# A one-core audio tower: x loaded in three parts, first heads split by batch, token statistics moved to GpSimd, and staged reads placed between the stores

## The chip, the cores and the metric

The kernel runs on one core of a Trainium2 chip. The time is the device time of one launch in microseconds. Before the change it is 169.0 us, the median of three runs (167.67 to 170.44).

## The reference

x is (16, 4000): 16 signals. Three stages follow each other; what is computed, cut to what matters:

```python
# 1 token stage: interpolate x by 4, windows of 64, 250 tokens of 64 per signal
kw = 0.5*(w + 1.3)**2 + 0.5*exp(-0.5*(w - 0.7)**2)
M = abs(fft(kw)); Mmax = M.max(-1)
h = soft_minimum(M * sigmoid(M - 0.12*Mmax), 0.9*Mmax)
# 2 attention, 8 heads of 64, sigmoid instead of softmax
q, k, v = (layernorm(h) @ W for W in (Wq, Wk, Wv))
h = h + relu((sigmoid(q @ k.T * 8) @ v) @ Wo)
# 3 shared MLP and 4 experts, two of them chosen by a softmax gate
y = layernorm(h)
out = h + shared(y) + sum_of_top2(gates(y), experts(y))
```

A token's 64 values are symmetric (bins 1 to 31 mirror 33 to 63), so the kernel works with 33 of them in stage 1 and with 32 folded features in the score and value products. The folded weights are products made on the chip.

## The kernel before

There are 16 signals, two to a **pair** g (0 to 7), each with 250 tokens in two interleaved halves of 125: four rows of `tok` to a pair, 32 in all. The rows are handled in groups `first` (0 to 7, pairs 0 and 1), `third` (8 to 15, pairs 2 and 3) and `later` (16 to 31, pairs 4 to 7). All engines run their own instruction lists, strictly in the written order, and meet at semaphores.

**Stage 1.** x comes as 36 taps by 2000 columns (`tapsT`), in two loads of 500 and 1500 columns (line 232), after memsets on VectorE (line 649) and GpSimd (line 1160). SyncE then issues the loads of the attention weights (233) and the FFN weights (234); ScalarE issues three loads of constants (1032 to 1034). Four quarters of 500 columns go through interpolation (TensorE, 289), square and exponential (ScalarE, 1040, 1042), two sums (VectorE, 653, 657) and the Fourier product (TensorE, 297). Magnitudes, masks and tokens follow (`over`, `distance`, `soft_minimum`), then a layer norm by the steps `total`, `centre`, `square`, `total`, `variance` (lines 711 to 732) on VectorE and a power of -0.5 on GpSimd (`inverse_deviation`, 1167), and the split of the normalised rows into two float16 parts (`split_rows`, 1172, on GpSimd; for pair 0 on VectorE, 750).

**Stage 2.** For a pair g: `x_transpose(g)` on TensorE, `x_take(g)` on VectorE copies to XT; then queries projected by head. For pair 0 this is `y_pair(p)` for four pairs of heads into banks 2 to 5 (372), whose high float16 part is taken by ScalarE (`pair_high`, 1090) and whose low part by VectorE (`pair_low`, 893). For other pairs it is `y_project(g, k)` for two halves of the heads k (361), `y_take(g, k)` on VectorE (769, 771), a store to DRAM (`send`, 242) and four reads that bring it back in another layout into YS (`read_back`, 255), all issued by SyncE in one order: store 0, store 1, reads 0, reads 1. Then there are eight units n for each pair: `scores(n)` (389 for pair 0, 398 else), the sigmoid on ScalarE (1110), `mix(n)` (418), emitted two units later; units 0 to 3 of a pair use the first half of the heads. `z_take(g, u)` copies what two units mixed. `mix` writes banks 4 and 5. The main loop (471) scatters the transposes, projections and `attn_out` of other pairs between the units.

**What ties pairs together.** `attn_out(g)` is added to the tokens by `add_attention(g)` on VectorE (782). It waits for `mirrored` 2: GpSimd copies the mirrored half of the tokens (1232) for rows 0 to 15 and then 16 to 31. `x_transpose(g)` for g >= 4 shares bank 7 with it and waits for `h2_done` >= g - 3 (344), that is for `add_attention(g - 3)`. GpSimd's list before the change: powers and split for pair 1, packing of the score weights, splitting of the FFN weights (1212 to 1224), powers and splits for pairs 2 and 3, one power for all later rows, the two mirrored copies, then splits of pairs 4 to 7 and the second layer norm (`norm2`).

**Stage 3** begins at about 105 us: layers 1 to 3 of the experts and the shared part on TensorE, pair by pair.

## Time and profile before

| what | value |
|---|---|
| median of three runs | 169.0 us |
| profiled execution: time, span | 168.07 us, 166.3 us |
| granted TensorE clock, mean | 0.974 |
| busy TensorE | 150.9 us (91%) |
| busy ScalarE, VectorE, GpSimd | 114.2, 109.5, 50.2 us |
| staged queries: stores, reads | 14 of 250 KB, 56 of 125 KB |

The profiled execution is the one that the rows come from; its time is the span and 1.77 us around it. A busy share over the whole span mixes the three stages; the stages are best read one by one, as the rows further down do. PE stands for TensorE, PEld for its weight loads, DVE for VectorE, ACT for ScalarE, POOL for GpSimd, SP for SyncE.

### The profile page before, as it was taken

How to read it: one execution, taken by the hardware profiler on the slowest of the kernel's cores; microseconds unless marked ns; L12 is line 12 of the kernel's file. 1: busy time of each engine (PE TensorE's matmuls, PEld its weight loads, DVE VectorE, ACT ScalarE, POOL GpSimd, SP SyncE). 2: the span in 40 equal slices, each digit the busy share in tenths (PEclk: the TensorE clock that was granted, in tenths of full speed). 3: DMA queues.
4: the chain of work that ended last, by engine and by line, in shares of the span. 5: the costliest groups of instructions: out<-in, count | busy, mean ns of one | idle time of the engine just before them, and what ended most of it. 6: DMA issues, size and time to landing. Idle time of an engine off the chain costs nothing.

```text
span 166.3 us, 6649 instructions
## 1 busy us (share of the span) xinstructions
PE 150.9 (91%) x2824; PEld 90.4 (54%) x2824; DVE 109.5 (66%) x277; ACT 114.2 (69%) x156; POOL 50.2 (30%) x94
## 2 busy tenths in 40 slices
PE   7799695996998999999989999999999999999890
PEld 2278531443454667575646455544666565765580
DVE  2396998996686767767681949777359884443521
ACT  3498973996877897978877898647636627457420
POOL 4000019692932855463416162526100000000000
PEclk9999659999999999999999999999999999999997
DMA  5920000058277685929576800000000100101002
GB/s 144 197 101 0 4 0 0 0 158 216 91 197 220 161 210 134 239 73 236 150 200 167 189 6 4 4 0 0 4 23 14 33 9 26 31 4 35 21 17 59
DMA packets 14701, 14.03 MB, mean 84 GB/s; under 512 B 1288, under 2 KB 14444, under 8 KB 14608
## 3 DMA queue, kind: packets, MB, share of 16 engines
q1 hardware_dynamic: 14240, 13.25, 30.5%
q8 instruction: 22, 0.36, 0.9%
q10 hardware_dynamic: 432, 0.36, 0.9%
q14 instruction: 7, 0.06, 0.1%
HBM read 9.00 MB, written 4.60 MB: 82 GB/s over the span
## 4 chain that ended last, share of the span: by engine, by line
PE 43%; DMA 21%; DVE 12%; SPq 11%; ACT 8%; issue 3%; DVEq 0%
DMA y_stage<-YP 14%; SPq L255 11%; PE ps L516 8%; PE ps L534 7%; PE ps L573 7%; PE ps L418 5%; PE ps L398 5%; DMA YS<-y_stage 4%; PE ps L543 3%; DMA area<-x_in 3%; PE ps L558 2%; PE ps L429 2%; ACT probs L1110 1%; PE ps L454 1%; ACT area L1046 1%
## 5 line engine op out<-in xcount | busy, mean ns | idle before, releaser
L1110 ACT ACTIVATE probs<-ps 125x1000 f32<-125x1000 f32 x64 | 61.6, 1007 | 11.8 <-PE ps L398 10.4
L418 PE MATMUL ps<-probs,xn 124*32 124x250 f32 (+1 forms) x512 | 39.0, 375 | 0.0
L398 PE MATMUL ps<-YS,XT 128*32 128x500 f16 x448 | 34.1, 376 | 3.4 <-DMA YS<-y_stage 3.2
L418 PEld LDWEIGHTS ps<-probs,xn 124*32 124x32 f32 (+1 forms) x512 | 15.6, 109 | 12.2 <-issue 1.5
L1140 ACT ACTIVATE H2r<-ps,wf 128x500 f32<-128x500 f32 x16 | 10.8, 677 | 15.4 <-PE ps L534 15.4
L779 DVE COPY ZS<-ps 128x250 f32<-128x250 f32 x32 | 12.9, 414 | 11.0 <-PE ps L418 10.8
L398 PEld LDWEIGHTS ps<-YS,XT 128*32 128x32 f16 x448 | 10.4, 96 | 12.3 <-DMA YS<-y_stage 4.5
L979 DVE TENSOR_TENSOR area<-H2r,ps 128x500 f32<-128x500 f32 x16 | 10.8, 674 | 9.2 <-ACT H2r L1140 8.6
L534 PE MATMUL ps<-area,wf 128*64 128x500 f32 x64 | 16.7, 585 | 0.0
L1127 ACT ACTIVATE area<-ps,wf 128x500 f32<-128x500 f32 x24 | 15.9, 672 | 0.9 <-PE ps L516 0.9
L1169 POOL TENSOR_TENSOR norm<-norm,half_neg 125x4 f32<-125x4 f32 (+1 forms) x5 | 6.9, 1397 | 26.7 <-DVE norm L732 26.7
L573 PE MATMUL ps<-wf,area 128*61 128x64 f32 (+1 forms) x384 | 14.0, 225 | 0.0
L573 PEld LDWEIGHTS ps<-wf,area 128*64 128x64 f32 (+1 forms) x384 | 13.2, 136 | 0.6
L970 DVE TENSOR_SCALAR area<-ps,wf 128x500 f32<-128x500 f32 (+1 forms) x16 | 9.5, 604 | 6.0 <-PE ps L516 5.8
L769 DVE CAST YP<-ps 128x500 f16<-128x500 f32 x12 | 8.1, 677 | 7.7 <-PE ps L361 7.7
L516 PE MATMUL ps<-X2T,w1h 128*64 128x500 f16 x64 | 12.9, 382 | 0.0
L516 PE MATMUL ps<-X2T,w1l 128*64 128x500 f16 x64 | 12.7, 373 | 0.0
L1186 POOL TENSOR_TENSOR lnsq<-ln 125x256 f32<-125x256 f32 x8 | 4.9, 612 | 25.3 <-DVE ln L796 25.3
L771 DVE TENSOR_TENSOR YP<-ps,YP 128x500 f16<-128x500 f32 x14 | 9.5, 678 | 1.0 <-issue 0.3
L279 PE MATMUL ps<-warm 128*128 128x512 f16 x20 | 8.2, 578 | 1.0 <-POOL warm L1159 1.0
L429 PEld LDWEIGHTS ps<-outW,ZS 128*32 128x32 f32 (+1 forms) x512 | 8.2, 109 | 1.5 <-issue 0.4
L429 PE MATMUL ps<-outW,ZS 128*32 128x64 f32 (+1 forms) x512 | 8.7, 219 | 0.0
(151 smaller groups left out, 247.6 us busy)
## 6 DMA issues: line engine op xcount, KB each, us to landing
YS<-y_stage SPq DMA_DIRECT2D x56, 125.0 KB, 3.0
y_stage<-YP SPq DMA_DIRECT2D x14, 250.0 KB, 4.0
tower_out<-res SPq DMA_DIRECT2D x8, 124.0 KB
wf<-wf_in SPq DMA_DIRECT2D x1, 648.0 KB, 7.3
wa<-wa_in SPq DMA_DIRECT2D x1, 512.0 KB, 6.5
area<-x_in SPq DMA_DIRECT2D x1, 210.9 KB
ch<-ch_in ACTq DMA_DIRECT2D x1, 160.0 KB, 4.9
cf<-cf_in ACTq DMA_DIRECT2D x1, 128.5 KB, 2.6
```

Source lines behind the costliest of these rows:

```text
L255: sp.dma_start(YS[row:row + R, g % 3, 4 * k:4 * k + 4, :], src).then_inc(y_in[g % 3][k], 16)
L398: last = mm(ps[k0:k1, 2 * (n % 2) + j, 0:TG].rearrange("p (h n) -> p h n", h=2), XT[:, g % 3, (2 * bb + cj) * P + k0:(2 * bb + cj) * P + k ...
L418: last = mm(ps[R * hh:R * hh + R, 4 + bb, half * TB:(half + 1) * TB], xn[0:keys, 4 * g + 2 * bb + cj, :], probs[0:keys, n % 3, hh, :], sta ...
L429: last = mm(ps[q0:q1, 7, t * F:(t + 1) * F], ZS[:, g % 2, half, t * P + q0:t * P + q1], outW[:, half, :], start=(half == 0), stop=(half == 1))
L516: last = mm(ps[F * c:F * c + F, n % 3, 0:TG], w[:, e * 128 + F * c:e * 128 + F * c + F], X2T[:, g, :], start=(k == 0), stop=(k == 1))
L534: last = mm(ps[F * j:F * j + F, 3 + k, 0:TG], wf[:, WF["w2"][0] + e * F:WF["w2"][0] + (e + 1) * F], H1[:, g % 2, e, :], start=True, stop=True)
L573: last = mm(ps[q0:q1, OUT_BANK[g], t * F:(t + 1) * F], H2[:, g % 2, k, t * P + q0:t * P + q1], wf[:, WF["w3"][0] + k * F:WF["w3"][0] + (k ...
L779: v.tensor_copy(ZS[:, g % 2, half, bb * TB:(bb + 1) * TB], ps[:, 4 + bb, half * TB:(half + 1) * TB]).then_inc(z_cp, 1)
L979: v.tensor_tensor(H2[:, g % 2, k, :], H2r[:, g % 2, k, :], ps[:, 5, 0:TG], ALU.mult).then_inc(mix_done, 1)
L1110: fn(probs[:, n % 3].rearrange("p (j h) n -> p j (h n)", j=2), ps[0:P, 2 * (n % 2):2 * (n % 2) + 2, 0:TG], ACT.Sigmoid, scale=SCORE_SCALE) ...
L1127: fn(H1[:, g % 2, e, :], ps[:, n % 3, 0:TG], ACT.Relu, bias=wf[:, WF["b1"][0] + e:WF["b1"][0] + e + 1]).then_inc(l1_act, 1)
L1140: fn(dst, src, ACT.Relu, bias=wf[:, WF["b2"][0] + k:WF["b2"][0] + k + 1]).then_inc(l2_act, 1)
```

## The change

Six things are done at once.

1. x comes in three loads (500, 500, 1000 columns). The loads of attention weights, `ch` (which ScalarE issued before) and FFN weights go out by SyncE behind the landing of the third.
2. For the first rows the variance step is gone: epsilon is added within `total`, the power is taken of the sum and a factor of 8 is multiplied in later.
3. The queries of pair 0 come in six parts: head pairs 0 and 1 are split by signal (parts 0 to 3, 250 columns, banks 2 to 5), head pairs 2 and 3 (parts 4 and 5, 500 columns, banks 4 and 5 again) are projected after unit 1. Their copies on ScalarE go behind sigmoids 1 and 2.
4. Projections and transposes for pairs 1 to 3 are placed up to two units earlier, `attn_out(0)` one later.
5. Tokens of the later rows and squares of the third and later rows are computed on GpSimd (VectorE and ScalarE before). Order on VectorE and GpSimd is new, as the diff shows: powers and splits of pairs 2 to 4 stand ahead of the splitting of the FFN weights.
6. SyncE's order is store 0 of a pair, reads 1 of the pair before, store 1, reads 0. In the FFN `layer3` of the last pair but one is emitted earlier.

The diff, cut to its core:

```diff
-PAIR_BANK = (2, 3, 4, 5)
+PARTS = ((0, 0, 2), (1, 0, 3), (0, 1, 4), (1, 1, 5), (2, None, 4), (3, None, 5))
+TAP_COLS = (slice(0, 4 * P), slice(4 * P, 8 * P), slice(8 * P, NB * P))
...
+            sp.wait_ge(taps_in[2], 16)
             sp.dma_start(wa[:], wa_in).then_inc(attn_w_in, 16)
+            sp.dma_start(ch[:], ch_in).then_inc(const16_in, 16)
...
-            for g in range(1, NG):
-                for k in range(2):
-                    send(g, k)
-                for k in range(2):
-                    read_back(g, k)
+            send(1, 0)
+            send(1, 1)
+            read_back(1, 0)
+            for g in range(2, NG):
+                send(g, 0)
+                read_back(g - 1, 1)
+                send(g, 1)
+                read_back(g, 0)
+            read_back(NG - 1, 1)
...
# TensorE
+            def y_part(i):
...
+                if i >= 4:
+                    pe.wait_ge(yd_lo, i - 1)
...
-                        pe.wait_ge(yd_lo, pair + 1)
+                        pe.wait_ge(yd_lo, (5 if half else 3 if bb else 1) + i)
...
-                if n == 0:
-                    pe.wait_ge(yd_lo, 3)
-                if n == 2:
-                    pe.wait_ge(yd_lo, 4)
+                if n in (0, 2):
+                    pe.wait_ge(yd_lo, 5 + n // 2)
...
-                if n in (0, 1):
-                    y_project(1, n)
-                if n == 6:
+                if n == 0:
+                    for k in range(2):
+                        y_project(1, k)
+                if n == 1:
+                    for i in (4, 5):
+                        y_part(i)
+                if n == 5:
                     x_transpose(2)
-                if n in (7, 8):
-                    y_project(2, n - 7)
-
-                if t == (3 if g == 1 else 1) and 1 <= g < NG - 2:
+                if n in (6, 7):
+                    y_project(2, n - 6)
+
+                if t == (2 if g == 1 else 1) and 1 <= g < NG - 2:
                     x_transpose(g + 2)
...
-                if t == (4 if g == 1 else 3) and g >= 1:
+                if t == (5 if g == 1 else 3) and g >= 1:
...
# VectorE
-            total(first, masked)
-            variance(first)
+            total(first, masked, F * EPS)
+            dve1_at["squares", first.start] = st.n
...
             x_take(0)
             total(third, tok)
+            for i in range(2):
+                part_low(i)
+            x_take(1)
+            for i in range(2, 4):
+                part_low(i)
             centre(third)
...
             y_take(1, 0)
+            dve.wait_ge(square_pool, 1)
             total(third, masked)
             variance(third)
+            part_low(4)
             y_take(1, 1)
+            part_low(5)
 
             z_take(0, 0)
-            soft_minimum(later)
+            x_take(2)
+            z_take(0, 1)
+            y_take(2, 0)
+            y_take(2, 1)
+            z_take(0, 2)
+            dve.wait_ge(token_pool, 1)
             total(later, tok)
...
             centre(later)
...
+            z_take(0, 3)
+            x_take(3)
+            z_take(1, 0)
+            y_take(3, 0)
+            dve.wait_ge(square_pool, 2)
             total(later, masked)
             variance(later)
...
# ScalarE, after sigmoid n
+                if n in (1, 2):
+                    part_high(n + 3)
                 if n in (0, 1):
                     second_high(n)
-                if n == 6:
-                    act.wait_ge(dve1, dve1_at["centred", later.start])
-                    fn(masked[:, later, :], mag[:, later, 0:NBIN], ACT.Square).then_inc(square_done, 1)
...
# GpSimd, behind the packing of the score weights
+            pool.wait_ge(act1, 6)
+            v.tensor_tensor(tok[:, later, 0:NBIN], masked[:, later, :], dist[:, later, :],
+                            ALU.subtract).then_inc(token_pool, 1)
...
+            square_rows(third)
+            inverse_deviation(slice(8, 12), third)
+            split_rows(2)
+            inverse_deviation(slice(12, 16), third)
+            split_rows(3)
+            square_rows(later)
+            inverse_deviation(slice(16, 20), later)
+            split_rows(4)
             pool.wait_ge(ffn_w_in, 16)
             v.tensor_copy(w1h[:], wf[:, 0:E * 128 + F + E]).then_inc(w1_split, 1)
...
-            inverse_deviation(slice(8, 12), third)
-            split_rows(2)
-            inverse_deviation(slice(12, 16), third)
-            split_rows(3)
-            inverse_deviation(later, later)
+            inverse_deviation(slice(20, 32), later)
+            pool.wait_ge(dve1, dve1_at["token", third.start])
             for rows in (slice(0, 16), later):
-                pool.wait_ge(dve1, dve1_at["token", later.start if rows == later else third.start])
                 v.tensor_copy(tok[:, rows, NBIN:F], tok[:, rows, NBIN - 2:0:-1]).then_inc(mirrored, 1)
```

## Rows read from the trace of the kernel before

**Rows 1.** Stage table: us; busy PE, PEld, DVE, ACT, POOL (count); clock; DMA share; GB/s.
```profile
59.00:105.00 46.00, 44.83 (x1160) 26.93 (x1145) 31.48 (x91) 39.44 (x45) 20.25 (x37) 1.00 0.55 141
```
**Rows 2.** Timeline, TensorE: starts of pairs 1 to 6 and x_transpose(4); start, us, instruction, idle before.
```profile
40.31 0.61 PE L398 MATMUL ps<-YS,XT 128*32 128x500 f16 x8 [1.31 <-DMA YS<-y_stage]
...
50.42 0.61 PE L398 MATMUL ps<-YS,XT 128*32 128x500 f16 x8 [0.92 <-DMA YS<-y_stage]
...
52.13 0.39 PE L350 MATMUL ps<-ch,xs 125*32 125x125 f16 x16
...
59.01 0.60 PE L398 MATMUL ps<-YS,XT 128*32 128x500 f16 x8
...
67.73 0.60 PE L398 MATMUL ps<-YS,XT 128*32 128x500 f16 x8
...
76.98 0.61 PE L398 MATMUL ps<-YS,XT 128*32 128x500 f16 x8 [0.35 <-DMA YS<-y_stage]
...
86.37 0.61 PE L398 MATMUL ps<-YS,XT 128*32 128x500 f16 x8 [0.63 <-DMA YS<-y_stage]
```
**Rows 3.** Timeline, the four quarters of the interpolation on TensorE and VectorE.
```profile
5.85 0.68 DVE L653 SCALAR_TENSOR_TENSOR area<-ps,square 128x500 f32<-128x500 f32 x1 [3.96 <-ACT square L1040]
6.40 2.78 PE L289 MATMUL ps<-area,cf 128*128 128x500 f32 x6 [1.21 <-DMA area<-x_in]
...
8.17 0.68 DVE L653 SCALAR_TENSOR_TENSOR area<-ps,square 128x500 f32<-128x500 f32 x1 [0.91 <-ACT square L1040]
...
9.48 0.67 DVE L653 SCALAR_TENSOR_TENSOR area<-ps,square 128x500 f32<-128x500 f32 x1
```
**Rows 4.** Timeline, the variance step on VectorE (third rows).
```profile
33.08 0.17 DVE L732 TENSOR_SCALAR norm<-norm 125x8 f32<-125x8 f32 x1
```
**Rows 5.** Timeline, first scores: VectorE's steps and TensorE's units of pair 0.
```profile
28.01 0.46 DVE L722 SCALAR_TENSOR_TENSOR mag<-norm,tok 125x264 f32<-125x264 f32 x1
...
28.39 1.25 DVE L893 TENSOR_TENSOR YS<-ps,YS 128x500 f16<-128x500 f32 x2
...
31.85 0.63 PE L418 MATMUL ps<-probs,xn 125*32 125x250 f32 x8
...
32.35 0.16 DVE L714 TENSOR_TENSOR norm<-masked 125x8 f32<-125x8 f32 x1
...
34.18 0.41 DVE L779 COPY ZS<-ps 128x250 f32<-128x250 f32 x1
...
35.11 0.64 PE L389 MATMUL ps<-YS,XT 64*125 64x250 f16 x8
...
36.24 0.64 PE L389 MATMUL ps<-YS,XT 64*125 64x250 f16 x8
```
**Rows 6.** Timeline, GpSimd: weight splitting (first, last), pair 3 (first, last), power, mirrored copies.
```profile
28.13 0.87 POOL L1212 CAST w1h<-wf 128x580 f16<-128x580 f32 x1
...
31.90 0.18 POOL L1224 COPY wg<-w1l 128x4 f16<-128x4 f16 x1
...
36.03 1.01 POOL L1169 TENSOR_TENSOR norm<-norm,half_neg 125x4 f32<-125x4 f32 x1
...
38.10 0.43 POOL L1182 TENSOR_TENSOR xs<-xn,xs 125x128 f16<-125x128 f32 x1
41.97 2.90 POOL L1169 TENSOR_TENSOR norm<-norm,half_neg 125x16 f32<-125x16 f32 x1 [3.44 <-DVE norm L732]
44.82 1.14 POOL L1232 COPY tok<-tok 125x496 f32<-125x496 f32 x2
```
**Rows 7.** TensorE's clock: stage table of 17.7 to 24.4, and timeline of three stretches.
```profile
17.70:24.40 6.70, 6.26 (x41) 3.40 (x42) 6.14 (x16) 6.11 (x11) 0.02 (x1) 0.50 0.01 2
...
18.14 1.98 PE L320 MATMUL ps<-wkT,wqT 64*128 64x64 f32 x16 [1.83 <-ACT wkT L1070]
...
0.98 3.38 PE L279 MATMUL ps<-warm 128*128 128x512 f16 x8 [0.98 <-POOL warm L1159]
...
27.31 1.02 PE L372 MATMUL ps<-XT,scoreW 128*128 128x500 f16 x4 [0.53 <-DVE XT L760]
```

More of the change, by code:

```diff
@@ L180, in build @@
             sem(s) for s in ("interp_in", "const_in", "const16_in", "attn_w_in", "ffn_w_in"))
-        taps_in = [sem(f"taps_in{q}") for q in range(2)]
+        taps_in = [sem(f"taps_in{q}") for q in range(3)]
         w16_set = sem("w16_set")
@@ L190, in build @@
         xn_pool = sem("xn_pool")
[L191 to L192 removed]
+        xs0_done, xs_pool, half_set, square_pool, token_pool, rstd_done = (
+            sem(s) for s in ("xs0_done", "xs_pool", "half_set", "square_pool", "token_pool", "rstd_done"))
         xt_mm, xt_cp, y_mm, y_hi, y_lo = (sem(s) for s in ("xt_mm", "xt_cp", "y_mm", "y_hi", "y_lo"))
@@ L363, in y_project @@
                 last.then_inc(y_mm, 1)
-            def y_pair(p):
-                if p == 0:
+            def y_part(i):
+                p, b, bank = PARTS[i]
+                cols = columns_of(b)
+                if i == 0:
                     pe.wait_ge(xt_cp, 1)
@@ L467, in _ @@
             x_transpose(0)
-            for p in range(4):
-                y_pair(p)
+            for i in range(4):
+                y_part(i)
             x_transpose(1)
@@ L601, in _ @@
                     layer2(g, 1)
+                if g == NG - 1:
+                    layer3(g - 1)
                 if g + 1 < NG:
@@ L617, in _ @@
                     layer1(g + 1, 3)
-                if 1 <= g <= NG:
+                if 1 <= g <= NG and g != NG - 1:
                     layer3(g - 1)
@@ L709, in soft_minimum, with total @@
                     v.tensor_tensor(tok[:, rows, 0:NBIN], masked[:, rows, :], dist[:, rows, :], ALU.subtract))
-            def total(rows, of):
+            def total(rows, of, plus=0.0):
                 st.wait()
-                st.done(v.tensor_tensor(norm[:, 1, rows], of[:, rows, 0], of[:, rows, R], ALU.add))
+                if plus:
+                    st.done(v.scalar_tensor_tensor(norm[:, 1, rows], of[:, rows, 0], -plus, of[:, rows, R],
+                                                   ALU.add, ALU.add))
+                else:
+                    st.done(v.tensor_tensor(norm[:, 1, rows], of[:, rows, 0], of[:, rows, R], ALU.add))
                 st.wait(st.done(v.tensor_reduce(norm[:, 0, rows], of[:, rows, 0:NBIN], AX_X, ALU.add)))
@@ L749, in _ @@
             dve.wait_ge(rstd_done, 1)
-            st.wait(st.done(v.tensor_tensor(xn[:, rows, :], mag[:, rows, 0:R], wide(4, rows, R, norm), ALU.mult)))
+            st.wait(st.done(v.scalar_tensor_tensor(xn[:, rows, :], mag[:, rows, 0:R], float(F) ** 0.5, wide(4, rows, R, norm),
+                                                   ALU.mult, ALU.mult)))
             high, low, full = parts(rows)
@@ L1086, in second_high, with part_high @@
                 fn(YP[:, 1, 0, k, :], ps[:, y_bank(1, k), 0:TG], ACT.Copy).then_inc(y_hi, 1)
-            def pair_high(p):
-                act.wait_ge(yd_mm, p + 1)
-                fn(YS[:, 0, 2 * p, :], ps[:, PAIR_BANK[p], 0:TG], ACT.Copy).then_inc(yd_hi, 1)
-            for p in range(4):
-                pair_high(p)
+            def part_high(i):
+                p, b, bank = PARTS[i]
+                cols = columns_of(b)
+                act.wait_ge(yd_mm, i + 1)
+                fn(YS[:, 0, 2 * p, cols], ps[:, bank, cols], ACT.Copy).then_inc(yd_hi, 1)
+            for i in range(4):
+                part_high(i)
             def gate_sigmoids(r):
@@ L1200, in norm2 @@
                                 ALU.subtract).then_inc(x2s_done, 1)
-            inverse_deviation(slice(0, 4), first)
-            inverse_deviation(slice(4, 8), first)
+            pool.wait_ge(dve1, dve1_at["squares", first.start])
+            for g in range(2):
+                rows = slice(4 * g, 4 * g + 4)
+                v.tensor_tensor(norm[:, 4, rows], norm[:, 2, rows], half_neg[0:P, rows], ALU.pow).then_inc(rstd_done, 1)
+            pool.wait_ge(rstd_done, 2)
+            v.tensor_scalar(norm[:, 4, 4:8], norm[:, 4, 4:8], float(F) ** 0.5, None, ALU.mult).then_inc(rstd_done, 1)
             split_rows(1)
@@ L1209, in _, with square_rows @@
                               scoreW[:, :, 0, :].rearrange("p (i a j) r -> p i a j r", i=2, a=2)[:, :, k]).then_inc(packed, 1)
+            pool.wait_ge(act1, 6)
+            v.tensor_tensor(tok[:, later, 0:NBIN], masked[:, later, :], dist[:, later, :],
+                            ALU.subtract).then_inc(token_pool, 1)
+            def square_rows(rows):
+                pool.wait_ge(dve1, dve1_at["centred", rows.start])
+                v.tensor_tensor(masked[:, rows, :], mag[:, rows, 0:NBIN], mag[:, rows, 0:NBIN],
+                                ALU.mult).then_inc(square_pool, 1)
+            square_rows(third)
[6 more added lines that the diff above has]
+            split_rows(4)
             pool.wait_ge(ffn_w_in, 16)
```

49 lines of the change are left out of this document (18 added, 31 removed).

## The prediction, made before the change was built or timed

> **What bounds the kernel now.** I read the stage table first, then the timelines of each stage. From 59 to 105 us TensorE is busy 44.83 of 46.00 us and ScalarE 39.44 [rows 1]: there the kernel runs at TensorE's pace. One batch pair (eight score units) takes 67.73 - 59.01 = 8.72 us [rows 2]. What is not at this pace are the starts of pairs whose staged queries are late: pair 1 at 40.31, pair 2 at 50.42, pair 5 at 76.98 and pair 6 at 86.37 all sit behind "DMA YS<-y_stage" [rows 2]. Pair 1 lasts 50.42 - 40.31 = 10.11 us, pair 5 9.39. Ahead of 40 us a chain over all engines sets the time. So I follow three things: the chain to the first scores, the start of each pair, and what other engine can hold TensorE in pairs 1 and 2. All clock times below are on the old time axis; what the head saves is taken off at the end. The sum is made against the profiled execution, 168.07 us, which lies 0.93 under the median of 169.0.
>
> **Head.** Quarter 2 of the interpolation waits for a large load until 6.40, though quarter 1 was at VectorE at 5.85 and quarter 2 got there at 8.17. The pitch of a quarter on VectorE is 9.48 - 8.17 = 1.31 [rows 3]. With a load of its own, quarter 2 comes at 5.85 + 1.31 = 7.16: **-1.0**. Bounds: 0 if the small load lands no sooner, -1.2 if ScalarE's part also shrinks; the load is of the size of the first, so I take -1.0. The weights now leave after x has landed; the first that uses them is two engines off the chain, so I cost that at nothing (worst case some 0.5). Dropping the variance step of the first rows takes 0.17 and a hand-over off the chain [rows 4]: **-0.2**. The extra multiply on GpSimd is behind the first power and off this chain. Head: **-1.2**.
>
> **First scores.** VectorE has finished its sums at 28.01; it now subtracts for two half-width parts before centring instead of after. A 250-column operation takes 0.41 against 0.63 for each of the two full ones, which ended at 28.39 + 1.25 = 29.64 [rows 5]; parts 0 and 1 are ready at 28.42 and 28.8, 0.85 sooner, and so is the first sigmoid. But this is not kept. Mix 0 writes bank 4, and bank 4 now also holds part 4, so mix 0 waits for VectorE's fifth subtraction. In front of that stand on VectorE: second copy x_take(1), parts 2 and 3, centring (to 30.2), y_take(1,0) (to 31.4), the nine tenths of a microsecond of total and variance (32.35 to 33.25 now [rows 4, 5]; then 31.45 to 32.35), and part 4, 0.68: 33.05. The squares of these rows, now GpSimd's, are done by 31.0 and hold nobody. Mix 0 ran at 31.85; it will run at 33.05, and behind it TensorE goes at its own pace of 36.24 - 35.11 = 1.13 per unit [rows 5]. Through units 3 to 7 with one transposition and two projections (0.33 + 0.2 + 0.2) the ninth scores come at 33.05 + 0.57 + 4 x 1.13 + 0.8 + 0.85 = **39.8**, against 40.31. The data are there: its first projection is stored 1.0 earlier, at 31.4. Gain here only 0.5, and it is overrun by what follows.
>
> **The copies that the attention sum waits for.** This is the step that I think decides. add_attention(0) waits for `mirrored` 2, the two mirrored copies of the tokens on GpSimd; x_transpose(4), the second unit of pair 2, waits for add_attention(0). Now the copies end at 44.82 + 1.14 = 45.96, and TensorE comes to x_transpose(4) at 52.13 [rows 2, 6]: no wait. In the new order two things happen.
> VectorE computes the variance of the later rows not at 41.9 but behind z_take(0,3), x_take(3), z_take(1,0) and y_take(3,0). y_take(2,1) ends at 41.4, z_take(0,2) 41.75, total 42.7, centring 43.4, z_take(0,3) 43.8, x_take(3) 44.15, z_take(1,0) 44.5. The projection for y_take(3,0) was held by x_take(3) and is there at 44.6; two passes of 0.68 take it to 46.0; total and variance 1.2 more: **47.2**.
> GpSimd then has, before the copies: power of 4 columns and split_rows(4), 38.53 - 36.03 = 2.5; all of the splitting of the FFN weights, which used to be done at 28 to 32 and is now queued behind split_rows(4), 32.08 - 28.13 = 3.95; the power of 12 columns, between 1.01 for 4 and 2.90 for 16, by their slope 2.27; the copies, 1.14 [rows 6]. That is 9.86. Copies end at 47.2 + 0.1 + 9.9 = 57.2; add_attention 0.42: x_transpose(4) can start at **57.6** instead of 52.13: **+5.5**. TensorE would have reached it at about 51.7 and stands for six microseconds. VectorE stands too, with z_take(1,3) and x_take(4) behind the wait. Bounds: 56.2 if the second VectorE chain follows the ninth scores with no other wait (their start plus 6.3, then 10), 58.6 if the GpSimd rows stretch as the cast did (0.29 to 0.65).
>
> **After the wait.** At full clock one more 0.7 is lost, as y_project(4,0) waits for x_take(4), which VectorE reaches 1.75 after its release. But the clock will not stay full. [...] How long it lasts once work is back has two rows: 6.3 us behind 18.14, and at the launch the eight warm-up matmuls of 512 columns still went at 0.42 each for 3.38 us (the clock's column reads full there, so I go by their pace), against 0.25 for 500 columns at full clock [rows 7]. Half of such a stretch is lost: 1.7 to 3.1, and this swallows the 0.7. I take **+2.4**; both ends, and 0.7 for no fall at all, go into the range.
> [...] The 0.42 and 0.25 above agree with a halved pace.
>
> **Order of stores and reads.** SyncE now issues four reads between two stores instead of standing until a store has landed. Pairs 5 and 6 no longer start late. Pairs 4 and 5 lasted 9.25 and 9.39 instead of 8.72 [rows 2]: **-1.2**. Against it: the second half of the reads of pair 1 waits behind the first store of pair 2, which is ready only at 40.1; four issues and a landing of about 3 us bring the data at 45.3, and unit 12 would start at 44.6. That 0.7 lies ahead of the long wait and adds nothing to it, as GpSimd's chain starts from VectorE. In later pairs each read is some ten microseconds early.
>
> **Tail.** layer3 of the last pair but one fills a hole of 0.44 us, but the last one waits for a spread that moves behind it by 0.9; nothing, within 0.3.
>
> **Sum.** 168.07 - 1.2 (head) + 5.5 (copies) + 2.4 (clock and resumption) - 1.2 (pairs 4, 5) = 173.6. The wait of pair 2 at 50.42 lies before 52.13 and is in the +5.5. With half of the 0.93 to the median: **174.0 us**.
>
> **Rivals.**
> 1. *Faster.* The copies are done by the time TensorE needs them. The place is add_attention(0) and the point from which it decides is 51.7: what leads from variance to copies would have to take 4.5 us, not 9.9, or be started 5 us sooner. Then pair 1 takes 8.5 from 39.8, pair 2 starts at 48.3 to 50.0 instead of 50.42: 168.07 - 1.2 - (0.4 to 2.1) - 1.2 = 163.6 to 165.3. For it: all other moves of the change are of this kind, and GpSimd is idle for 3.44 before the power [rows 6]. Against it: both queues are strictly in order, and five of the ten microseconds cannot overlap.
> 2. *The wait, but the clock holds or comes back at once.* +0.7 instead of +2.4: 171.9, with the offset 172.3, on the bound. The row of 1.83 us idle speaks against it.
> 3. *The wait is half as long*, because the weights split faster with VectorE standing (those rows had VectorE busy beside them) and variance comes earlier: x_transpose(4) at about 55, a smaller fall of the clock: about 170.5.
> 4. *The change doesn't do what it says* for the head: x lands no sooner. Then 1.0 more, 175.0.
>
> **Chances.** The forecast case (173 to 175) with the head failing included 0.66, rival 2 0.14, rival 3 0.10, rival 1 0.10. What can be told from no change is about 2%, 165.6 to 172.4. Faster 0.10; same 0.20 (rival 3, most of rival 2, a little of the first); slower 0.70. The range goes from 170.0 (rival 3) to 176.5 (174.0 with clock at +3.1, start at 58.6 and a head that saves less); rival 1 and the edges are left out. The likeliest case's own range is 172 to 176.
>
> **What would show it.** Power on 16 columns gone, the mirrored copies at 55 to 57 (less 1.2, so 54 to 56) right behind the weight splitting; VectorE idle for some six microseconds before add_attention, released by GpSimd; a hole of five to six in TensorE in pair 2 and a clock of 0.5 behind it; no "DMA YS<-y_stage" wait from pair 2 on; quarter 2 at VectorE at about 7.2. Wrong if VectorE does not wait for GpSimd there: then rival 1.

## The result, and the profile after

The changed kernel takes **173.8 us** (median of four runs, 173.67 to 174.59) against 169.7 us for the kernel before (four runs on the same chip): 1.034 times as long, with a 95% interval of 1.025 to 1.042. This ratio and all below leave out the executions that took over 1.5% more than the fastest of the same kernel (here 170.41 and 170.44 of the kernel before), while the medians are over all executions, so a ratio is not the quotient of two medians. The profiled execution took 173.71 us with a span of 171.9 us, 5.64 over the profiled execution before. The likeliest case came: 174.0 had been said.

The page of the changed kernel first: busy time (share of the span) by engine, then the granted clock in 40 slices of 4.3 us.

```profile
PE 154.5 (90%) x2826; PEld 92.8 (54%) x2826; DVE 108.1 (63%) x276; ACT 114.2 (66%) x157; POOL 53.1 (31%) x99
...
PEclk9999759999879699999999999999999999999999
```

This page alone misleads twice. TensorE is *more* busy, 154.5 against 150.9 us, though its matmuls are the same kind of work: at a granted clock of 0.50 the same eight matmuls count for more, 1.05 us at 47.29 against 0.61 at 45.77 (timeline below). And the shares hardly move, though five microseconds were lost. The slices with 8, 7 and 6 in the middle are the place. The stage table (columns as in [rows 1]: busy time of each engine with counts, clock, DMA share, GB/s) shows two stretches at a granted clock of 0.50 there, and then a long one at 1.00 in which TensorE is idle for only 0.18 of 40 us:

```profile
46.50:49.50 3.00, 3.00 (x50) 1.56 (x45) 0.30 (x2) 1.94 (x2) 2.65 (x5) 0.50 0.93 252
56.80:60.00 3.20, 3.20 (x46) 1.63 (x45) 2.27 (x6) 1.00 (x1) 1.82 (x3) 0.50 0.03 8
70.00:110.00 40.00, 39.82 (x1011) 24.36 (x1003) 27.64 (x81) 34.73 (x38) 16.60 (x31) 1.00 0.50 132
```

TensorE's timeline (start, duration, instruction, idle before it and what ended that) has the answer to [rows 2, 5]: the first transposition, mix 0, the start of pair 1, unit 12, the last mix before the hole, x_transpose(4), then the starts of pairs 3 to 7.

```profile
25.72 0.47 PE L362 MATMUL ps<-ch,xs 125*32 125x125 f16 x16 [0.56 <-DVE xs L778]
...
32.53 0.63 PE L432 MATMUL ps<-probs,xn 125*32 125x250 f32 x8 [1.65 <-DVE YS L920]
...
39.28 0.61 PE L414 MATMUL ps<-YS,XT 128*32 128x500 f16 x8
...
45.77 0.61 PE L414 MATMUL ps<-YS,XT 128*32 128x500 f16 x8 [1.79 <-DMA YS<-y_stage]
...
47.29 1.05 PE L414 MATMUL ps<-YS,XT 128*32 128x500 f16 x8
...
53.33 0.61 PE L432 MATMUL ps<-probs,xn 124*32 124x250 f32 x8
56.68 0.61 PE L362 MATMUL ps<-ch,xs 125*32 125x125 f16 x16 [2.75 <-DVE h L811]
57.06 1.07 PE L414 MATMUL ps<-YS,XT 128*32 128x500 f16 x8
...
65.18 0.60 PE L414 MATMUL ps<-YS,XT 128*32 128x500 f16 x8
...
73.90 0.60 PE L414 MATMUL ps<-YS,XT 128*32 128x500 f16 x8
...
82.62 0.60 PE L414 MATMUL ps<-YS,XT 128*32 128x500 f16 x8
...
91.34 0.60 PE L414 MATMUL ps<-YS,XT 128*32 128x500 f16 x8
...
101.07 0.60 PE L414 MATMUL ps<-YS,XT 128*32 128x500 f16 x8
```

The hole ends at 56.68, released by VectorE's add_attention (L811). One engine further, on VectorE, the add itself waited for GpSimd; the row above it is the variance of the later rows, and the last GpSimd rows are the chain between the two, which answers to [rows 6]. VectorE:

```profile
46.38 0.18 DVE L756 TENSOR_SCALAR norm<-norm 125x16 f32<-125x16 f32 x1
...
56.11 0.42 DVE L811 SCALAR_TENSOR_TENSOR h<-ps,tok 125x256 f32<-125x256 f32 x1 [3.49 <-POOL tok L1278]
```

GpSimd, same kernel:

```profile
46.63 1.01 POOL L1198 TENSOR_TENSOR norm<-norm,half_neg 125x4 f32<-125x4 f32 x1 [2.61 <-DVE norm L756]
...
48.92 0.67 POOL L1262 CAST w1h<-wf 128x580 f16<-128x580 f32 x1
...
52.48 0.18 POOL L1274 COPY wg<-w1l 128x4 f16<-128x4 f16 x1
52.62 2.29 POOL L1198 TENSOR_TENSOR norm<-norm,half_neg 125x12 f32<-125x12 f32 x1
54.87 1.14 POOL L1278 COPY tok<-tok 125x496 f32<-125x496 f32 x2
```

Power of four columns, a split, the weight splitting (48.92 to 52.66), power of twelve, copies: 9.38 us in a row behind a variance that itself came 4.7 later than before (46.38 against 41.72). The 1.14 us of copies need nothing of all this.

**The ledger**, from starts in the two profiles: x_transpose(0) 25.72 - 26.37 = -0.65. x_transpose(4) 56.68 - 52.13 = +4.55, so +5.20 beyond the head. From there to pair 3: 8.50 against 6.88, +1.62. Pairs 3 to 5 take 8.72 each (82.62 + 8.72 = 91.34) against 8.72, 9.25 and 9.39: -1.20. Pair 6 takes 9.73 against 9.41: +0.32. The rest of the span +0.3. That makes the 5.6.

### The profile page after: what moved, and what is told of

It is laid out like the page before. It is cut to its first block, busy times and chain, and to the rows that moved or that the text cites. A ratio compares the mean times of both kernels' runs of the same rounds, so it can differ in the third digit from the quotient of the medians.

```text
span 171.9 us, 6660 instructions
## 1 busy us (share of the span) xinstructions
PE 154.5 (90%) x2826; PEld 92.8 (54%) x2826; DVE 108.1 (63%) x276; ACT 114.2 (66%) x157; POOL 53.1 (31%) x99
## 4 chain that ended last, share of the span: by engine, by line
PE 67%; DVE 13%; ACT 8%; POOL 5%; issue 4%; DVEq 0%; POOLq 0%
PE ps L432 14%; PE ps L414 12%; PE ps L534 8%; PE ps L552 7%; PE ps L591 6%; PE ps L443 4%; PE ps L561 3%; PE ps L576 2%; PE ps L291 2%; POOL norm L1198 2%; PE ps L405 2%; DVE norm L739 2%; PE ps L373 1%; ACT area L1070 1%; ACT probs L1140 1%
## 5 line engine op out<-in xcount | busy, mean ns | idle before, releaser
L432 PE MATMUL ps<-probs,xn 124*32 124x250 f32 (+1 forms) x512 | 40.9, 386 | 1.7 <-DVE YS L920 1.6
L414 PE MATMUL ps<-YS,XT 128*32 128x500 f16 x448 | 35.9, 389 | 1.9 <-DMA YS<-y_stage 1.8
L432 PEld LDWEIGHTS ps<-probs,xn 124*32 124x32 f32 (+1 forms) x512 | 16.6, 112 | 14.8 <-issue 5.2
L414 PEld LDWEIGHTS ps<-YS,XT 128*32 128x32 f16 x448 | 11.3, 99 | 10.7 <-ACT probs L1140 4.1
L1156 ACT ACTIVATE area<-ps,wf 128x500 f32<-128x500 f32 x24 | 15.9, 672 | 0.9 <-PE ps L534 0.9
L591 PE MATMUL ps<-wf,area 128*64 128x64 f32 (+1 forms) x384 | 14.2, 225 | 0.0
L591 PEld LDWEIGHTS ps<-wf,area 128*61 128x61 f32 (+1 forms) x384 | 13.3, 136 | 0.8 <-issue 0.3
L443 PEld LDWEIGHTS ps<-outW,ZS 128*32 128x32 f32 (+1 forms) x512 | 8.8, 114 | 1.8 <-issue 0.9
L291 PE MATMUL ps<-warm 128*128 128x512 f16 x20 | 8.8, 614 | 1.0 <-POOL warm L1188 1.0
L1169 ACT ACTIVATE area<-ps,wf 128x500 f32<-128x500 f32 x8 | 5.4, 679 | 5.1 <-PE ps L561 5.1
```

The lines of the kernel that those rows point to most:

```text
L291: mm(ps[:, 0, :].rearrange("p (a n) -> p a n", a=4), warm[:], warm[:].unsqueeze(1).broadcast_to([128, 4, 128]), start=True, stop=True)
L414: last = mm(ps[k0:k1, 2 * (n % 2) + j, 0:TG].rearrange("p (h n) -> p h n", h=2), XT[:, g % 3, (2 * bb + cj) * P + k0:(2 * bb + cj) * P + k ...
L432: last = mm(ps[R * hh:R * hh + R, 4 + bb, half * TB:(half + 1) * TB], xn[0:keys, 4 * g + 2 * bb + cj, :], probs[0:keys, n % 3, hh, :], sta ...
L443: last = mm(ps[q0:q1, 7, t * F:(t + 1) * F], ZS[:, g % 2, half, t * P + q0:t * P + q1], outW[:, half, :], start=(half == 0), stop=(half == 1))
L591: last = mm(ps[q0:q1, OUT_BANK[g], t * F:(t + 1) * F], H2[:, g % 2, k, t * P + q0:t * P + q1], wf[:, WF["w3"][0] + k * F:WF["w3"][0] + (k ...
L1156: fn(H1[:, g % 2, e, :], ps[:, n % 3, 0:TG], ACT.Relu, bias=wf[:, WF["b1"][0] + e:WF["b1"][0] + e + 1]).then_inc(l1_act, 1)
```

## The experiments

The time of each kernel is a median; its ratio is to the kernel before, run beside it on the same chip.

**Is it the weight splitting in front of the copies?** The splitting block on GpSimd is moved behind the second layer norm of pair 1.

```diff
-            pool.wait_ge(ffn_w_in, 16)
-            v.tensor_copy(w1h[:], ...)
...
             inverse_deviation(slice(20, 32), later)
...
                 norm2(g - 1)
+                if g == 2:
+                    pool.wait_ge(ffn_w_in, 16)
+                    v.tensor_copy(w1h[:], ...)
...
```

> The changed kernel, with GpSimd's splitting of the FFN weights moved from ahead of the 12-column power to behind norm2(1); nothing else. In the changed kernel the splitting takes 48.92 to 52.66, the mirrored copies end at 56.01 and x_transpose(4) starts at 56.68, 3 us after TensorE had run out of work (53.8). Theory (the late copies hold TensorE, and the idle time lowers its clock): copies end at about 52.3, x_transpose(4) starts at 53.8 to 54.0 with nothing waited for, the clock stays at 1.00 from 54 to 62, and the time falls by 2.8 + 1.6 = 4.4 us, to about 169.3, no longer distinguishable from the kernel before. Rival A (the order of SyncE's stores and reads is what costs; the copies only fill a wait that is there anyway): x_transpose(4) moves but a wait for the reads takes its place, time within 1 us of 173.7. Rival B (the clock's fall in pair 1, 46 to 49.6, is the loss): also within 1 us of 173.7.

Measured: **170.62 us**, ratio 1.009 (1.004 to 1.014) instead of 1.034: some three quarters of the loss are gone. In GpSimd's timeline the copies follow the power directly:

```profile
50.09 2.27 POOL L1198 TENSOR_TENSOR norm<-norm,half_neg 125x12 f32<-125x12 f32 x1
52.30 1.15 POOL L1264 COPY tok<-tok 125x496 f32<-125x496 f32 x2
```

and TensorE's hole before x_transpose(4) is 0.53 instead of 2.75, with the clock at 1.00 behind it (54 to 58). Of what is left, this 0.53 and some 0.4 of resumption behind it come from the late variance and the power, which still stand ahead of the copies. The rest lies before them in this profile: unit 12 waits 1.96 us for its reads, and the clock was at 0.50 from 32.2 to 35.6, behind mix 0, which puts the variance 1.1 us later than in the changed kernel. So the 53.8 without a wait that was expected for x_transpose(4) did not come (54.13, behind a wait).

**Only the copies ahead.** The two copies alone go ahead of the squares of the later rows.

```diff
+            pool.wait_ge(dve1, dve1_at["token", third.start])
+            for rows in (slice(0, 16), later):
+                v.tensor_copy(tok[:, rows, NBIN:F], ...)
             square_rows(later)
...
             inverse_deviation(slice(20, 32), later)
-            pool.wait_ge(dve1, dve1_at["token", third.start])
-            for rows in (slice(0, 16), later):
-                v.tensor_copy(tok[:, rows, NBIN:F], ...)
```

> The changed kernel with the two mirrored copies alone moved ahead of the squares of the later rows, where GpSimd is idle; the weight splitting stays between split_rows(4) and the 12-column power. If it is the copies that VectorE's add_attention(0) waits for, and not the splitting or the power behind them, this single move gives all that moving both gave: x_transpose(4) no longer waits, ratio to the kernel before about 1.00 (0.998 with both moved), 3.5% less than the changed kernel. If something else of GpSimd's list also holds TensorE there (the split of pair 4, the weights), a wait stays: 1.01 to 1.03.

Measured: **170.17 us**, ratio 1.011 (1.006 to 1.015). The copies stand at 36.8 and nobody waits for them. So moving three lines takes the ratio from 1.034 to 1.011. That gain is smaller than the expected one (to 1.00), and not for the reason given for such a case: x_transpose(4) waits for nothing of GpSimd's. Its profile, GpSimd and then TensorE, has the copies and the next wait, unit 12 behind the reads of pair 1:

```profile
36.80 1.14 POOL L1260 COPY tok<-tok 125x496 f32<-125x496 f32 x2
```
```profile
47.30 1.02 PE L414 MATMUL ps<-YS,XT 128*32 128x500 f16 x8 [3.02 <-DMA YS<-y_stage]
...
55.12 0.41 PE L362 MATMUL ps<-ch,xs 125*32 125x125 f16 x16
```

Behind this idle time too the granted clock was 0.50, from 47.3 to 50.3 (stage table), and the eight matmuls took 1.02 us instead of 0.61.

**Splitting and copies ahead.** Both go into GpSimd's idle stretch, behind the split of pair 3 and ahead of the squares.

```diff
+            <weight splitting, mirrored copies>
             square_rows(later)
             inverse_deviation(slice(16, 20), later)
             split_rows(4)
-            <weight splitting>
             inverse_deviation(slice(20, 32), later)
-            <mirrored copies>
```

> The changed kernel with both the weight splitting and the two mirrored copies placed in the stretch in which GpSimd is idle (36.6 to 43.0), behind split_rows(3) and ahead of the squares of the later rows; the 12-column power stays behind split_rows(4). Theory: copies end at about 41.5, so they hold nobody, and the gain is the same 4.4 us as with the splitting alone moved, about 169.3, since TensorE has work until 53.8 in both. If the splitting in this place slows VectorE's casts and sums beside it, the variance comes later and the gain is up to 1 us less. Rivals A and B: within 1 us of 173.7.

Measured: **169.62 us**, ratio 0.998 (0.993 to 1.003). The whole loss is gone, and x_transpose(4) runs at 53.25. What is left before it is again unit 12, in TensorE's timeline, and the clock, in the stage table:

```profile
45.27 0.79 PE L414 MATMUL ps<-YS,XT 128*32 128x500 f16 x8 [1.65 <-DMA YS<-y_stage]
```
```profile
45.50:49.50 4.00, 4.00 (x84) 2.16 (x80) 1.07 (x5) 2.02 (x2) 3.01 (x5) 0.57 0.99 241
```

**What does the low clock cost?** The changed kernel as it is, with 13 idle matmuls of 512 columns into a bank that nobody reads there, placed where TensorE would stand.

```diff
+                if n == 17:
+                    pe.wait_ge(y_lo, 6)
+                    for _ in range(13):
+                        mm(ps[:, 6, :]..., warm[:], ..., start=True, stop=True)
                 if t == (2 if g == 1 else 1) and 1 <= g < NG - 2:
```

> The changed kernel with 13 matmuls of 512 zero columns on TensorE ahead of x_transpose(4) (into bank 6, results never read). They fill the wait for the copies, 53.8 to 56.7, without changing what is waited for. Theory on the clock: x_transpose(4) starts at the same 56.7, the granted clock stays at 1.00 from 56.8 to 60.0 where it was 0.50, and pair 3 starts 1.6 us sooner (65.2 less 1.6), time about 172.1. If only the standing costs and the lowered clock is hidden behind the sigmoids: no difference, 173.7. If the 13 matmuls (0.216 each, 2.8 us) overrun the wait: up to 0.3 of it lost.

Measured: **172.69 us**, ratio 1.021 (1.014 to 1.029). The wait of VectorE for GpSimd is there as before (3.43 us), x_transpose(4) starts within 0.13 us of where it did, and only the pace behind it differs (timeline, then stage table):

```profile
53.64 2.98 PE L505 MATMUL ps<-warm 128*128 128x512 f16 x13
56.55 0.40 PE L362 MATMUL ps<-ch,xs 125*32 125x125 f16 x16
```
```profile
56.50:60.00 3.50, 3.43 (x121) 2.15 (x124) 3.35 (x8) 2.02 (x2) 2.04 (x4) 1.00 0.03 7
```

Pair 3 starts at 63.70, 7.15 behind x_transpose(4) instead of 8.50: the clock costs **1.35 us**, and the other 7.15 - 6.88 = 0.27 are resumption at full clock. Half of the stretch of 3.2 us that the changed kernel spends at 0.50 (56.8 to 60.0) would be an estimated 1.6; the runs show 1.35.

**Reads ahead of the next store.** On top of the kernel with splitting and copies ahead, the second half of pair 1's reads is issued before the first store of pair 2.

```diff
             read_back(1, 0)
-            for g in range(2, NG):
+            read_back(1, 1)
+            send(2, 0)
+            send(2, 1)
+            read_back(2, 0)
+            for g in range(3, NG):
```

> The kernel with copies and splitting in the idle stretch, and in addition the second half of pair 1's reads issued ahead of the first store of pair 2 (stores 0 and 1 of pair 1, its reads 0 and 1, stores 0 and 1 of pair 2, reads 0 of pair 2, then alternating as in the changed kernel). In the changed kernel unit 12 waits 1.79 us for these reads, until 45.77, and the clock is at 0.5 from 46.4 to 49.7. Theory: reads 1 are issued at about 36 to 38, unit 12 starts at 43.9 (held by y_project(3,0) alone), no clock fall in pair 1: 1.9 + 1.6 = 3.5 us more, about 165.8 us, 2 to 3% faster than the kernel before. Against it: stores of pair 2 come later by up to 0.5 and pair 2 could start late on its reads (now at 52.05); then the gain is 1 to 2 us. If the order of stores is of no account once the copies are early: no change from the kernel with early copies.

Measured: **167.00 us**, ratio 0.988 (0.984 to 0.993): a gain, but a smaller one than expected. Unit 12 no longer waits and the clock stays at 1.00 (42 to 50), but two smaller waits take back some of it:

```profile
40.33 0.61 PE L418 MATMUL ps<-YS,XT 128*32 128x500 f16 x8 [0.57 <-DMA YS<-y_stage]
...
44.19 0.60 PE L418 MATMUL ps<-YS,XT 128*32 128x500 f16 x8
...
46.09 0.40 PE L377 MATMUL ps<-XT,scoreP 128*32 128x500 f16 x4 [0.87 <-DVE YP L800]
```

The second, for VectorE's y_take(3, 0), is one that the long wait had covered. The first, at the start of pair 1, is not: the profiles of the changed kernel and of the four above that keep its order of reads have no wait there, and all six with the new order have one, of 0.23 to 0.65 us. The second half of the reads now goes out right behind the first; whether that is what holds the first up was not tried.

**The two small placements.** First layer3 of the last pair but one goes back to its old place, then attn_out(0) and the second projection of pair 3 change places, each on top of the one before.

```diff
-                if g == NG - 1:
-                    layer3(g - 1)
...
-                if 1 <= g <= NG and g != NG - 1:
+                if 1 <= g <= NG:
```

> The kernel with copies and splitting early and all reads of pair 1 ahead of pair 2's stores (167.0 us), with layer3 of pair 6 back at its old place behind layer2(7, 2). The profile of the changed kernel shows the spread and layer2(7, 2) 1.6 us later by it, and TensorE then waits 0.89 for ScalarE before layer3(7). Theory: 0.3 us less. The prediction had it at 0 within 0.3. Rival: 0.3 us more, since the hole of 0.44 comes back.

```diff
-                if t == 4 and 1 <= g < NG - 2:
+                if t == (5 if g == 1 else 4) and 1 <= g < NG - 2:
                     y_project(g + 2, 1)
...
-                if t == (5 if g == 1 else 3) and g >= 1:
+                if t == (4 if g == 1 else 3) and g >= 1:
```

> As the one with layer3 back, and in addition attn_out(0) behind unit 12 and y_project(3, 1) behind unit 13 (they are the other way round in the changed kernel). y_project(3, 1) waits 0.87 us there for VectorE's low part of y_take(3, 0), since both use bank 6; attn_out(0) has all it needs at 43.9. Theory: 0.9 us less than the one before it in this list, about 165.8 us if the other gives 166.7. Against it: y_take(3, 1) comes a microsecond later, and with it the add_attention(0) that x_transpose(4) waits for; then 0 to 0.5.

Measured: 166.30 (ratio 0.984, 0.980 to 0.988) and **165.66 us** (0.982, 0.978 to 0.986). The intervals overlap, so the two steps rest on the profiles. From the last pair's two final mixes (102.54 without the first step, 102.87 with it) to the end of the span there are 62.43 us instead of 62.76. With the second step the wait for VectorE (0.87 us, and 0.74 in the profile with layer3 back) is gone, with attn_out(0) in its place:

```profile
44.51 0.60 PE L436 MATMUL ps<-probs,xn 125*32 125x250 f32 x8
44.93 1.30 PE L447 MATMUL ps<-outW,ZS 128*32 128x64 f32 x62
```

**Can mix 0 start sooner?** The prediction held that total and variance stand ahead of part 4 on VectorE and so hold mix 0. They go behind it.

```diff
+            part_low(4)
             dve.wait_ge(square_pool, 1)
             total(third, masked)
-            variance(third)
-            part_low(4)
             y_take(1, 1)
+            variance(third)
             part_low(5)
```

> The fastest version so far (copies and splitting early, all reads of pair 1 ahead of pair 2's stores, layer3 back, attention sum and projection swapped; ratio 0.982), and in addition VectorE's subtraction for part 4 ahead of the total of the third rows, the variance behind y_take(1, 1). The prediction said that mix 0 waits for this subtraction behind 0.9 us of total and variance; in the changed kernel mix 0 waits 1.65 us until 32.53 for it. Theory: part 4 starts when ScalarE has its high part (31.6 in the time of the changed kernel), mix 0 goes 0.2 to 0.3 us earlier, and TensorE's chain to pair 1 with it, but y_take(1, 1) no sooner: 0.1 to 0.3 us less in all. Rival: pair 1 waits for its reads anyway (0.5 us), so 0.

Measured: 167.33 us, ratio 0.992 (0.989 to 0.995), on another chip than the 0.982; so both kernels were run once more, on one chip.

> The version of e7_swap_projection once more, on one chip with the version that has part 4 first; their ratios (0.982 and 0.992) came from different chips. If part 4 first really costs 1%, the two differ by that here too; the traces give no cause for more than 0.3 us either way, so the theory is that both come out within 0.5% of each other, at 0.98 to 0.99.

> The version of e9b_part4_first once more, beside the version without that step. Theory: within 0.5% of it. Rival: 1% above it, since y_project(3, 1) and the later variance come half a microsecond later.

Measured: 166.66 (0.983, 0.978 to 0.988) without and 166.86 (0.987, 0.982 to 0.992) with the edit: no difference that can be told. The reason is a row of VectorE, followed by one of TensorE, in the kernel with the edit:

```profile
32.07 0.68 DVE L922 TENSOR_TENSOR YS<-ps,YS 128x500 f16<-128x500 f32 x1 [0.63 <-ACT YS L1122]
```
```profile
32.90 0.63 PE L436 MATMUL ps<-probs,xn 125*32 125x250 f32 x8 [1.55 <-DVE YS L922]
```

With nothing in front of it, part 4 now waits for ScalarE, whose high part stands behind sigmoid 1. Mix 0 still waits 1.55 us, 0.1 less than without the edit.

**The parts that should help, each alone on the kernel before.** The new order of stores and reads:

```diff
-            for g in range(1, NG):
-                for k in range(2):
-                    send(g, k)
-                for k in range(2):
-                    read_back(g, k)
+            <the order of the reads-first kernel above>
```

> The kernel before, with SyncE's order alone changed: stores 0 and 1 and reads 0 and 1 of pair 1, stores 0 and 1 and reads 0 of pair 2, then from pair 3 on store 0, reads 1 of the pair before, store 1, reads 0. Theory: the late starts of pairs 5 and 6 go (pairs 4 and 5 last 8.72 instead of 9.25 and 9.39, 1.2 us), and pair 2's start at 50.42 moves little, since its reads 0 wait for a store that is only ready at 44.2: total -1.2 to -1.6 us, about 0.8% faster. Rival: in a kernel without other changes SyncE's lag is carried by later buffers anyway and only the place of the wait moves: 0 to -0.4 us.

Measured: 168.76 us, ratio 0.997 (0.993 to 1.000). The pairs do what was said, pair 5 (77.27) and pair 6 (85.99) start without a wait:

```profile
51.24 0.61 PE L406 MATMUL ps<-YS,XT 128*32 128x500 f16 x8 [1.05 <-DMA YS<-y_stage]
...
68.55 0.60 PE L406 MATMUL ps<-YS,XT 128*32 128x500 f16 x8
...
77.27 0.60 PE L406 MATMUL ps<-YS,XT 128*32 128x500 f16 x8
...
85.99 0.60 PE L406 MATMUL ps<-YS,XT 128*32 128x500 f16 x8
```

Pair 4 starts at 68.55 and pairs 4 and 5 take 8.72 each. This profile's head is 0.71 late (x_transpose(0) at 27.08), which hides the gain in its span. Counted from x_transpose(0) on, the profile is 0.91 us shorter than the one before: 1.07 less from pair 3 to pair 7, since pair 6 takes 9.55 instead of 9.41, and small losses elsewhere. The runs give some 0.5 us, with an interval that reaches 1.1. So it is less than the 1.2 to 1.6 that were expected, but how much less one can't tell.

The three loads of x, with the constants behind them:

```diff
-            for i, cols in enumerate((slice(0, 4 * P), slice(4 * P, NB * P))):
+            for i, cols in enumerate((slice(0, 4 * P), slice(4 * P, 8 * P), slice(8 * P, NB * P))):
...
+            sp.wait_ge(taps_in[2], 16)
             sp.dma_start(wa[:], wa_in).then_inc(attn_w_in, 16)
+            sp.dma_start(ch[:], ch_in).then_inc(const16_in, 16)
```

> The kernel before, with the three x loads, the weights behind them and ch issued by SyncE, nothing else. Forecast of the prediction for this part: -1.0 us. From the profile of the changed kernel and its variants, in which the first quarter reaches VectorE at 6.2 to 7.0 instead of 5.85 and only 0.1 to 0.6 was left of the gain: -0.1 to -0.6 us. In the profile, VectorE's sums of the four quarters should follow each other at 1.31 with no gap after the first, and x_transpose(0) should start at 25.8 to 26.3 instead of 26.37.

Measured: ratio 0.988 (0.983 to 0.994), more than was expected, but it rests on three of seven executions (166.75 to 167.50). The other four took 169.62 to 170.55, and the median of all seven is 169.62, against 169.40 for the kernel before: these runs don't settle the size. The profile is of one of the four (169.94). In it the sums of the quarters follow each other at 1.30 to 1.32 us, as expected, but x_transpose(0) starts at 26.44, outside the 25.8 to 26.3, because ScalarE's first square started at 6.50 instead of 5.23. From that square to x_transpose(0) it took 19.94 us, against 21.14 in the kernel before: the loads are worth 1.20 us on this chain, and the later start took it all back.

## Why the prediction was right

**Head, -1.2; measured -0.65 in the profile.** The pitch was right: quarter 2 follows quarter 1 after 1.33 us. But the first quarter itself was later, against 5.85 in [rows 3] (VectorE, kernel after):

```profile
6.61 0.68 DVE L673 SCALAR_TENSOR_TENSOR area<-ps,square 128x500 f32<-128x500 f32 x1 [4.71 <-ACT square L1068]
...
7.94 0.67 DVE L673 SCALAR_TENSOR_TENSOR area<-ps,square 128x500 f32<-128x500 f32 x1
```

So quarter 2 came at 7.94, not at 7.16. Over the eleven profiles of kernels with the whole new head, x_transpose(0) starts at 25.15 to 26.25, mean 25.74; over the two with the old head at 26.37 and 27.08, mean 26.73. That is -1.0, near the -1.2. One start can't give this term, but the chain from ScalarE's first square to x_transpose(0) can: 21.14 us before, 19.94 with the loads alone, and 19.73 to 19.76 in all eleven. So the loads gave 1.20 where 1.0 was said, the variance step its 0.2, and what is missing is the first square, which came 0.76 later (5.99 against 5.23): -1.41 + 0.76 = -0.65.

**First scores.** Mix 0 started 6.81 behind x_transpose(0) (said: 33.05 - 26.37 = 6.68), pair 1 13.56 behind it (said 13.4). The place was right and one cause was not: the runs with part 4 first show that it is also held by ScalarE's order, so with total and variance out of the way mix 0 came only 0.09 us sooner (6.65 behind x_transpose(0) instead of 6.74).

**Copies, +5.5; measured +5.20.** Variance was to end at 46.0 on the new axis (47.2 less the head) and ended at 46.56; GpSimd's chain was said to take 9.86 and took 9.38, so the copies end at 56.01 as said (57.2 - 1.2 = 56.0), from two small errors that cancel. The splitting was quicker than its rows of before, its cast 0.67 instead of 0.87 [rows 6]; the power of 12 columns took 2.29 where the slope gave 2.27. Moving the copies alone took the ratio from 1.034 to 1.011: this cause is shown.

**What was wrong here** is how long TensorE stands: 2.75 us, not six. The step that failed is "TensorE would have reached it at about 51.7", which is 50.5 once the head is taken off. It ran out of work only at 53.9, 3.4 later: pair 1 started 0.7 later than said (39.28 against 38.6), unit 12 waited 1.79 us (0.7 was said), and the clock was then 0.50 for 3.4 us, which the prediction had not foreseen and which costs an estimated 1.6 by the two paces of the next paragraph (0.83 and 0.43 us for eight matmuls). The reads that unit 12 waits for stand behind the first store of pair 2 in SyncE's timeline:

```profile
39.58 0.52 SPq L250 DMA_DIRECT2D y_stage<-YP  x1
40.15 2.06 SPq L263 DMA_DIRECT2D YS<-y_stage  x4
42.25 0.52 SPq L250 DMA_DIRECT2D y_stage<-YP  x1
```

The four were issued from 40.15 to 42.21, and unit 12, which waits for them, starts at 45.77, 3.6 after the last. None of this lengthened the run, since x_transpose(4) was set by GpSimd's chain: one wait lay inside the other. With the copies ahead it is no longer covered: that kernel waits 3.02 us at unit 12, and its profile reaches x_transpose(4) 29.05 us behind x_transpose(0), against 25.76 before the change. That the reads' place behind the store is the cause is shown by the kernel that moves them: unit 12 does not wait there.

**Clock and resumption, +2.4; measured +1.62.** The clock fell behind the wait as said (0.50 from 56.6 to 60.0), and the size was taken too large: with TensorE at work the low stretch lasted 3.3 us behind the wait and not the 6.3 of [rows 7]. That cost 1.35 by the run with the idle matmuls, and the resumption 0.27 instead of 0.7. That half of a low stretch is lost was the author's estimate; by that run it is 1.35 of 3.3, some four tenths. The lower end, 1.7 from the launch row, was the better choice. The prediction's 0.42 and 0.25 give a pace of 1.6 to 1 and not of 2 to 1; the 0.25 is a quarter of a row of 1.02 us that runs from the first start to the last end. Distances between starts show it better: eight matmuls take 0.83 us from 57.06 to the next mix at 57.89, and 0.43 from 52.90 to 53.33, 1.9 to 1.

**Order of stores and reads, -1.2; measured -1.20** in this profile (pairs 4 and 5 at 8.72). By itself on the kernel before it gave some 0.5 in the runs (0 to 1.1). No start of a pair waits for staged queries any more. Pair 6 took 0.32 more than before (9.73 against 9.41). In the eleven profiles with the new head it takes 9.55 to 10.42, and 9.55 also with the order alone changed, so 0.14 of this comes with a pair that starts without a wait; the rest differs from profile to profile.

**Tail, 0; measured +0.3**, the edge of what was said: layer3 of the last pair waits 0.89 us for a relu of ScalarE (TensorE's timeline), and with the old placement 0.33 came back.

```profile
166.04 0.22 PE L587 MATMUL ps<-b3s,WT 72*64 72x64 f16 x2 [0.89 <-ACT area L1169]
```

**The sum.** -1.2 + 5.5 + 2.4 - 1.2 = +5.5 was said and -0.65 + 5.20 + 1.62 - 1.20 + 0.3 + 0.3 = +5.6 measured. The head was 0.55 short and the clock term 0.8 too large; pair 6 and the tail made up most of the balance. The closeness of 174.0 to 173.8 is partly luck.

**The rivals.** Rival 1 (faster, copies in time) was wrong for this change; with another order on GpSimd the copies are in time, but the kernel is only as fast as before (169.6 and 170.2 us), since the wait of unit 12 comes out. Near its 163.6 to 165.3 comes only the best version below. Rival 2 (the clock holds) fell, and the run with the idle matmuls put its price at 1.35. Rival 3 (half the wait) fell too: the weights did split a little faster, the whole chain by 0.5 us, not by the 2.6 it needed (x_transpose(4) at 55 instead of 57.6). Rival 4 (x lands no sooner) fell: quarter 2 followed at the pitch, and what was lost in the head was lost ahead of the first square.

**The best version** has the change's order with splitting and copies ahead, pair 1's reads first, layer3 in its old place and the projection swapped: 165.7 us at 0.982 (0.978 to 0.986) of before, and 0.983 (0.978 to 0.988) on another chip. With the block on GpSimd moved the change is even with the kernel before (0.998); the order of pair 1's reads brought most of the rest.

## What to carry to other kernels

When work is handed to an engine that looks idle, write its queue out and ask of each short instruction behind it who waits for it and when; here 1.14 us of copies stood behind 8.2 us that they did not need. A wait inside a longer wait costs nothing and shows only once the longer one is gone (here unit 12's, 1.79 us inside and 3.02 once the copies were ahead), so mend in that order, and look at the profile again after each. And a stop of TensorE is priced with the slow stretch behind it where there is one (here 1.35 us behind a stop of 2.75), from a row of the same kernel, the shortest such row as well as the longest.

## What the runs showed of the hardware

- The same idle time of TensorE was followed by a granted clock of 0.50 in one profile and not in another. Idle times of 1.83 (kernel before), 1.79 (after) and 1.65 us (splitting and copies ahead) had 0.50 behind or around them; 1.96 us before the same unit 12, in the kernel with the splitting later, did not: its stage table from 47 to 50 us reads

```profile
47.00:50.00 3.00, 2.91 (x104) 2.00 (x108) 1.36 (x5) 2.02 (x2) 2.00 (x4) 1.00 0.96 277
```

- In that same profile the clock was 0.50 a little earlier, from 32.2 to 35.6, behind 1.64 us idle before mix 0. Seven other profiles have 1.64 or 1.65 us there and stayed at 1.00 (32 to 36). The pace of mix 0 shows it, first in the kernel with the splitting later, then with splitting and copies ahead:

```profile
32.18 1.06 PE L432 MATMUL ps<-probs,xn 125*32 125x250 f32 x8 [1.64 <-DVE YS L920]
```
```profile
32.09 0.63 PE L432 MATMUL ps<-probs,xn 125*32 125x250 f32 x8 [1.65 <-DVE YS L920]
```

- The low stretch, at a clock of 0.50, lasted 3.4 us twice in the changed kernel (46.4 to 49.8 and 56.6 to 60.0). In the weight stage it lasted 3.4 us in one kernel (splitting and copies ahead, 18.3 to 21.7) and 6.8 us in another (before, 17.7 to 24.5), there with TensorE at work without a break from 18.14 on: the 0.44 us that are missing in [rows 7] (6.26 of 6.70) lie ahead of that. So work alone did not end it sooner.
- The launch varies: ScalarE's first square starts between 5.23 and 6.51 us over 14 profiles. It is at 5.23 and 5.56 in the two with the old loads and at 5.40 to 6.51 in the twelve with the new ones; whether the new loads cause part of this stays open. The pace of TensorE goes with it: with the square at 5.40 its weight loads for the first quarters follow each other at 0.42 us from 4.78 on, with the square at 6.51 two of them are still 0.83 apart (5.44 and 6.27), though the clock's column reads 1.00 in both (4 to 7 us). A spread of 1.3 us in one profile's head can come from there.
- Four reads queued behind a store: unit 12 could start 5.6 to 5.8 us after the first of the four was issued in four kernels, and 6.9 us after in the one with the copies alone ahead, for the same bytes.
- In seven of the 14 profiles TensorE stands for 0.2 to 0.6 us in the middle of the 64 matmuls of an attn_out, waiting for nothing that the profile shows (0.59 us before 70.94 in the second profile of the best version). The profiles before and after the change have no such stop. It is part of why the pairs of one kernel differ between profiles, and its cause was not tried.
